# Layer normalisation by block inside attention's steps, in a two-layer attention and mixture-of-experts kernel

## The reference

```python
def _layernorm(x, axis=-1, eps=1e-05):
    m = jnp.mean(x, axis=axis, keepdims=True)
    v = jnp.var(x, axis=axis, keepdims=True)
    return (x - m) / jnp.sqrt(v + eps)

# attention: 16 heads of 16; layer 0 turns q and k by a rotary table, layer 1 has a padding mask
q = query @ Wq.T + bq;  k = ctx @ Wk.T + bk;  v = ctx @ Wv.T + bv
out = softmax(q k^T / 4) v                      # by head
return out @ Wo.T + bo

# experts of layer 0: 8, the best 2 of a row's router logits, and one shared expert of 512
h = (x @ W1[e]) * silu(x @ W3[e]);  y += w[e] * (h @ W2[e])
# experts of layer 1: 16 of 128, the best 4 by sigmoid scores within the best 2 of 4 groups,
# and a shared one of 256

x = x + xattn0(_layernorm(x), ctx);  x = x + ffn0(_layernorm(x))
x = x + xattn1(_layernorm(x), ctx);  x = x + ffn1(_layernorm(x))
```

## Time and profile before

| | us |
|---|---|
| median of 3 runs | 1056.0 |
| the runs | 1051.7, 1056.0, 1056.29 |
| the profiled execution, its own time | 1050.59 |
| its span, first to last instruction | 1048.8 |
| PE busy in the span | 910.7 |
| DVE busy | 671.4 |
| ACT busy | 471.4 |
| POOL busy | 321.3 |

### The profile page before, as it was taken

The page is one execution under the profiler, slowest core; times in us unless marked ns, Lnnn a source line. Parts: engine busy times, 40 slices in busy tenths (PEclk is TensorE's granted clock), DMA queues, the critical chain, the costliest instruction groups (busy, mean ns, idle before and its releaser), DMA issues.

```text
span 1048.8 us, 21972 instructions
## 1 busy us (share of the span) xinstructions
PE 910.7 (87%) x8517; PEld 801.9 (76%) x8517; DVE 671.4 (64%) x1398; ACT 471.4 (45%) x790; POOL 321.3 (31%) x262
## 2 busy tenths in 40 slices
PE   2689888579959999999845999986999999999997
PEld 2578677448859999999834788764778888888886
DVE  5756565477636777777654445546876666666666
ACT  6234445544317777666544554547222222322322
POOL 2321330223745676766421003002112121212210
PEclk9889999889979999999965999997999999999998
DMA  4406600102246888988550000002000000001002
GB/s 138 118 2 186 169 2 2 67 1 86 81 146 182 231 239 231 239 230 236 117 150 21 2 22 2 2 2 61 15 16 19 26 30 15 30 15 30 15 0 81
DMA packets 46115, 85.48 MB, mean 82 GB/s; under 512 B 6240, under 2 KB 33120, under 8 KB 45920
## 3 DMA queue, kind: packets, MB, share of 16 engines
q0 software_dynamic: 14784, 46.44, 16.5%
q1 hardware_dynamic: 31264, 38.09, 12.3%
HBM read 63.73 MB, written 20.79 MB: 81 GB/s over the span
## 4 chain that ended last, share of the span: by engine, by line
PE 66%; DVE 13%; ACT 10%; issue 6%; POOL 3%; DMA 2%; DVEq 0%; POOLq 0%; ACTq 0%
PE bank L1180 36%; PE bank L1216 9%; PE bank L1275 5%; PE bank L1373 3%; PE bank L1379 3%; PE bank L1346 3%; POOL sorted_x L400 2%; ACT prob L635 2%; ACT xn L515 2%; PE bank L1412 2%; PE bank L1422 2%; DMA w_raw<-in_fw,w_idx 1%; DVE qk L1020 1%; DVE rope_b L1020 1%; DVE shift L755 1%
## 5 line engine op out<-in xcount | busy, mean ns | idle before, releaser
L357 POOL TENSOR_TENSOR w_hi<-w_raw,zero_col 128x768 fp32r<-128x768 f32 (+1 forms) x20 | 31.9, 1597 | 357.0 <-PE bank L1216 234.8
L1180 PE MATMUL bank<-xT_hi,w_hi 128*128 128x512 f32 x352 | 139.1, 395 | 2.2 <-DVE hid L958 2.2
L1180 PE MATMUL bank<-xT_lo,w_hi 128*128 128x512 f32 x352 | 139.0, 395 | 0.0
L1180 PE MATMUL bank<-xT_hi,w_lo 128*128 128x512 f32 x352 | 138.8, 394 | 0.0
L945 DVE SCALAR_TENSOR_TENSOR xres<-bank,gate,xres 128x256 f32<-128x256 f32 x320 | 132.7, 475 | 1.2 <-PE bank L1216 1.2
L958 DVE TENSOR_TENSOR hid<-bank,act_sb 128x512 f32<-128x512 f32 x88 | 60.8, 691 | 105.7 <-ACT act_sb L584 105.4
L584 ACT ACTIVATE act_sb<-bank 128x512 f32<-128x512 f32 x88 | 52.6, 598 | 165.9 <-PE bank L1180 165.9
L1180 PE MATMUL bank<-xsT_hi,w_hi 128*128 128x256 f32 x368 | 106.9, 290 | 2.0 <-DVE xsT_lo L912 1.5
L1216 PE MATMUL bank<-w_hi,hid_hi 128*128 128x256 f32 x352 | 100.3, 285 | 6.2 <-DVE hid_lo L966 6.1
L1180 PE MATMUL bank<-xsT_lo,w_hi 128*128 128x256 f32 x368 | 103.8, 282 | 0.0
L1180 PE MATMUL bank<-xsT_hi,w_lo 128*128 128x256 f32 x368 | 103.8, 282 | 0.0
(11 more groups left out here) (199 smaller groups left out, 2277.9 us busy)
## 6 DMA issues: line engine op xcount, KB each, us to landing
w_raw<-in_fw SPq DMA_DIRECT2D x18, 384.0 KB, 3.0
sorted_x<-empty_row SPq DMA_DIRECT2D x2, 2967.0 KB, 20.1
xs<-sorted_x SPq DMA_DIRECT2D x23, 258.0 KB
ctx_raw<-in_ctxT SPq DMA_DIRECT2D x8, 512.0 KB, 4.5
summed<-empty_row SPq DMA_DIRECT2D x1, 2304.0 KB, 26.8
xres<-in_x SPq DMA_DIRECT2D x4, 512.0 KB, 5.9
aw_raw<-in_aw SPq DMA_DIRECT2D x8, 256.0 KB, 5.2
xn_all<-summed SPq DMA_DIRECT2D x4, 512.0 KB, 5.5
```

The source lines that it names most:

```text
L1180: last = nc.tensor.matmul(dst, lh, rh, start=(i == 0), stop=(i == len(pairs) - 1))
```

## The change

The table `build_at` is now written in one pattern: for m = 0, 1, 2 the steps 4m, 4m+1 and 4m+2 make K, Q and V of block m+1 (two items each), and steps 3 and 7 turn the rows of block 2 and 3 for the layer's own normalisation (X0, X1: four transposes each, where other items stand). The functions for a normalisation are split into parts for one block: `deviation`, `normal`, `high` (ACT), `statistics`, `scales`, `low` (DVE) and `rows_turned` (PE). Ahead of attention only blocks 0 and 1 are normalised. The new names of `next_norm(b)` say that steps 12, 13 and 15 turn blocks 0, 1 and 2 for the feed-forward. After attention only block 3 is left. The router's products of blocks 0 and 1 stand in step 16. In the first unit of experts, the products up(0,0) are issued before the last block's transposes; its weights are loaded when attention's K, Q and V are made and split by POOL from step 13 on.

Beside this: the mask's place in memory is moved, so that its load waits for nothing; the four weight loads of layer 1 stand ahead of the loads of the experts' sums; the sort's parts on DVE come with every half step of the shared expert (`between(ls, j)`); the tiles' weights use four semaphores where two were, POOL no longer waits for w_hi before it fetches a tile's weights, and the first two tiles' weights are fetched between the two rounds of scatters.

The core of the diff:

```diff
         def build_at(b):
-            early = {0: (1, K0, K1), 1: (1, Q0, Q1), 2: (1, V0, V1)}
-            if b in early:
-                return early[b]
-            n, s = divmod(b, BLK)
-            if s == 3 and n + 2 < NBLK:
-                return n + 2, K0, V0
-            if s == 0 and n + 1 < NBLK:
-                return n + 1, K1, V1
-            if s == 1 and n + 1 < NBLK:
-                return n + 1, Q0, Q1
+            m, s = divmod(b, BLK)
+            if b == 3 or b == 7:
+                return m + 2, X0, X1
+            if m + 1 < NBLK and s < 3:
+                return (m + 1,) + ((K0, K1), (Q0, Q1), (V0, V1))[s]
             return None
+        def next_norm(b):
+            return {12: 0, 13: 1, 15: 2}.get(b)
...
@@ SP @@
-                sp.wait_ge(a["xadd"], B)
+                sp.wait_ge(a["vps"], 2 * NBLK)
+                sp.wait_ge(a["proj"], 4 * NBLK)
                 for par in range(2):
                     sp.dma_start(w_raw[:, par, 0:768 * J], fw[l][par + (0 if l else SHARED), :, :]).then_inc(f[f"w_in{par}"], 16)
...
@@ POOL, the sort @@
-                    if j:
-                        pool.wait_ge(TS["w_hi"], 2 * j + h - 1)
...
-                for h in range(2):
-                    tile_weights(0, h)
                 pool.wait_ge(LN["ln_xn"], 2 * B)
                 for r in range(2):
                     if r:
+                        for j in range(2):
+                            for h in range(2):
+                                tile_weights(j, h)
                         pool.wait_ge(TS["scatter"], 16 * B)
...
@@ POOL, attention @@
+                    if b == 13:
+                        pool.wait_ge(a["turn"], 12)
+                        split_unit(f, 0, 0, 768 * JT[l])
-                pool.wait_ge(a["xadd"], B)
-                for par in range(2):
-                    split_unit(f, 0, par, 768 * JT[l])
+                pool.wait_ge(a["turn"], B)
+                split_unit(f, 0, 1, 768 * JT[l])
...
@@ ACT, end of step b of attend @@
+                        if made and made[1] == X0:
+                            high(2 * l, made[0])
+                        if next_norm(b) is not None:
+                            high(2 * l + 1, next_norm(b))
+                        if l == 1 and b == 1:
+                            deviation(2, 2)
+                            deviation(2, 3)
-                        if b in (2, 5):
+                        if b in (2, 6):
+                            normal(2 * l, 2 + b // 4)
                             context_high(2 + b // 4)
+                        if b == 10:
+                            if l == 0:
+                                act.wait_ge(s_vset, 3)
+                            deviation(2 * l + 1, 0)
+                            deviation(2 * l + 1, 1)
+                        if b in (11, 12):
+                            normal(2 * l + 1, b - 11)
+                        if b == 13:
+                            deviation(2 * l + 1, 2)
+                        if b == 14:
+                            normal(2 * l + 1, 2)
+                        if b == B:
+                            router_copy(l, 0)
+                            router_copy(l, 1)
...
@@ DVE, end of step b of attend, behind the residual @@
+                        if b in (3, 7):
+                            low(2 * l, 2 + b // 4)
+                        if next_norm(b) is not None:
+                            low(2 * l + 1, next_norm(b))
+                        if l == 1 and b < 2:
+                            tiles_back(2 + b)
+                            statistics(2, 2 + b)
+                        if l == 1 and b == 2:
+                            scales(2, 2)
+                            scales(2, 3)
+                        if l == 0 and b == 6:
+                            first_constants()
+                        if b == 10:
+                            next_statistics(0)
+                            next_statistics(1)
+                        if b == 11:
+                            scales(2 * l + 1, 0)
+                            scales(2 * l + 1, 1)
+                        if b == 13:
+                            next_statistics(2)
+                        if b == 14:
+                            scales(2 * l + 1, 2)
...
@@ PE, attend, behind weighed @@
+                        if next_norm(b) is not None:
+                            pe.wait_ge(a["exp"], NG * b + 1)
+                            rows_turned(2 * l + 1, next_norm(b), 0)
+                        if b == B:
+                            pe.wait_ge(s_wsplit[l], 2)
+                            pe.wait_ge(LN["ln_lo"], 2 * (NBLK * (2 * l + 1) + NBLK - 1))
+                            router_products(0)
...
@@ ACT, then DVE, behind attend @@
-                ln_act(2 * l + 1, (lambda n, t: xn[:, n % 2, t, :]) if l else (lambda n, t: xn_all[:, BLK * n + t, 0:D]))
+                deviation(2 * l + 1, NBLK - 1)
+                router_copy(l, 2)
+                normal(2 * l + 1, NBLK - 1)
+                high(2 * l + 1, NBLK - 1)
+                router_copy(l, 3)
-                ln_dve(2 * l + 1, lambda n: dve.wait_ge(a["xadd"], BLK * (n + 1)))
+                next_statistics(NBLK - 1)
+                scales(2 * l + 1, NBLK - 1)
+                low(2 * l + 1, NBLK - 1)
```

359 lines of the change are left out of this document (197 added, 162 removed).

## The result

The changed kernel is slower: 1065.4 us (median of 7 runs, 1062.7 to 1069.1) against 1054.4 (7 runs, 1051.0 to 1056.3), a ratio of 1.011 with a 95% interval of 1.0084 to 1.0137. Its profiled execution took 1067.61, its span is 1065.8, and the mean granted clock fell from 0.946 to 0.937.

A forecast was written before the change was run, and what follows sets the result against it. TensorE was taken as the apparent bound, with ACT and DVE just behind at step ends. Layers -4.9 and -1.2 plus clock +13.3 gave +7.2: 1057.8 us as profiled, 1063 as median, range 1043 to 1079.

The forecast's parts named there:

- The likeliest case: Whole kernel: late step ends lower TensorE's clock, +3 to +14 us, 1059 to 1070; chance 0.40.
- start of attention: Ahead of attention: fewer blocks normalised first, so it starts earlier, -4.8 us in layer 0 and -12.5 in layer 1.
- behind attention: Feed-forward normalisation and router after attention: one block's chain stays, -15.0 us in layer 0 and -13.1 in layer 1.
- Where the pieces surface: Steps 10 to 14: normalisation work at step ends exceeds ACT's and DVE's slack, +14.6 us in each layer.
- The collision with w_lo: Step 11, layer 0 only: DVE's scales meet GpSimd's weight split, +1.8 us (0 to 2.6).
- The table loads: ACT's loads around each std: costed at nothing; four uncovered switches would add 10.6 us to each layer.
- The clock: Attention: late steps' waits bring TensorE's lower clock, seven net periods of 1.9 us, +13.3 (0 to about 28).
- Steps 15 and 16: End of attention: transposes of block 2 and eight router products, +1.7 us in each layer.
- The signs: Changed profile: first-label wait near 6 us, attention some 20 longer per layer, oT_lo waits of 2.4 or more.
- The clock unchanged: Rival, whole kernel: gain kept without a clock loss, -6 us, 1042 to 1055, centre 1050; chance 0.27.
- The work really hides: Rival, attention: late steps cost only TensorE's own transposes, some 8 us; about -43, 1013; chance 0.08.
- Slower by much: Rival: two half-clock periods per late step or more shift waits, +14 to +28 us, 1070 to 1084; chance 0.17.

The follow-up runs named there:

- e4: The changed kernel with unneeded products added in front of the oT_lo waits of steps 11 to 15, both layers: 1056.1 us.
- e1: The changed kernel with feed-forward statistics, scales, roots and normal of blocks 0 to 2 moved from step ends to where ACT and DVE wait: 1032.4 us.
- e2: As e1, with the attention's own normalisation of blocks 2 and 3 moved as well: 1021.6 us.
- e8: The kernel before, with two added copies on ACT in front of oT_hi in steps 11 to 14, both layers: 1055.8 us in one run.
- e6: The changed kernel with GpSimd's split of the first unit's weights started one step later: 1087.0 us in one run.
- e12: As e11, with unneeded products added in front of the waits of steps 2, 5, 6, 7, 9 and 10 of layer 0: 1020.2 us.
- e11: As e2, with GpSimd's weight fetches in the old order, the first tile's ahead of the first scatter round: 1027.7 us.
- e9: The changed kernel, unedited, measured again in a later session: 1093.9 us, ratio 1.040 to the kernel before.
- e10: The kernel of e2, unedited, measured again in a later session: 1049.2 us, ratio 0.995 to the kernel before.

## Why the prediction was right, point by point

The likeliest case came, at 1065.4 against 1063, and the mechanism was the one forecast: the pieces surface at the ends of steps, and the waits that they make lower TensorE's clock. The number is closer than the sum behind it, which missed 10 us of 17; that part is luck, and so is the session, since the same kernel took 1093.9 in a later one. The terms, each read from the trace of the changed kernel against that of before:

| term | predicted, layer 0 / 1 | measured |
|---|---|---|
| start of attention | -4.8 / -12.5 | -3.9 / -12.0 |
| behind attention (layer 1: to the end of the program) | -15.0 / -13.1 | -14.9 / -12.2 |
| sort, from the ranks to the first tile | -3.4 | -4.0 |
| tile stage | -2.5 | -2.1 |
| behind attention, layer 1, up to the next products of the unit | -13.1 | -13.1 |
| step 11 at full clock (e4) | +4.4 / +2.6 | +4.6 / +2.3 |
| steps 12 to 14 at full clock (e4) | +8.6 / +8.6 | +8.1 / +8.4 |
| steps 15 and 16 at full clock (e4) | +1.7 / +1.7 | +1.6 / +1.6 |
| clock, steps 11 to 14 | within 13.3 for all | +5.2 / +8.1 |
| clock, steps 15 and 16 | within 13.3 for all | +1.6 / +1.4 |
| both attentions in all | +45.2, clock +13.3 | +66.1 |

**Where the pieces surface.** Right, and shown: e1 and e2 keep every instruction and lose 33 and 44 us. The slack was read rightly to 0.3 us (e8). The measured steps 11 to 14 at full clock (e4) are within 0.3 of the sums for single steps, and step 10, put down as +3.4, grew by 3.7 in layer 0 (12.47 against 8.79).

**The collision with w_lo.** Right: shift took 2.16, 2.0 more than its 0.16, where 1.8 was put down; without it the step is 2.0 shorter (e6).

**The table loads.** Put at nothing, and nothing shows. ACT around the loads of step 11 in e1:

```profile
162.97 0.48 ACT L507 ACTIVATE std<-meanvar,eps_col 128x4 f32<-128x4 f32 x2
163.47 1.28 ACT L637 ACT_TABLE_LOAD   x1
164.76 0.69 ACT L637 ACTIVATE prob<-bank,zero_col 128x512 f32<-128x512 f32 x1
```

The load takes 1.28, with no more than 0.02 us free on either side. The 2.66 a switch that the prediction quotes is not seen here, so even four uncovered switches would cost 5.1 a layer and not 10.6.

**The clock.** The mechanism was right and shown by e4 and again by e12 against e11. The price was right too: in steps 11 to 14 seven of the eight ran slow and lost 1.3 to 2.5 each against e4, 13.3 in all and 1.9 apiece, as was put down; the eighth, step 14 of layer 0, ran at 0.99 behind a wait of 2.79. That these seven alone make the forecast's 13.3 is luck, for its seven were to be all the slow periods there are. What was mis-sized is their number. The two steps 15 lost 1.6 and 1.4 more. In layer 0 steps 5, 7 and 9 ran at 0.86, 0.81 and 0.86 and took 12.41, 9.17 and 12.37, against 10.8, 7.8 and 10.8 at full clock (e12), some 4.5 us that were in no term. In layer 1 steps 2 and 3 were slow as forecast (0.87 and 0.84); step 3 took 9.07 against 7.70 at full clock (e2). Waits of 2.2 us as before steps 5, 6, 9 and 10 were there in before too (2.18 in the earlier trace rows), and I took them as harmless; here two of the four were followed by the lower clock. The count of one in four was of layer 0 alone, and a wait of 2.16 at the start of layer 1's attention in before was followed by half clock as well:

```profile
567.08 1.84 PE L1346 MATMUL bank<-k_full,q_half 32*128 32x128 f32 x32 [2.16 <-ACT q_half L626]
```

The same 32 take 1.17 at full clock. Outside attention the clock took some of the gains back: behind the wait of 5.72 before the ranks, and of 2.20 in layer 1, twelve products in a row took about 0.63 apiece where they took about 0.40 before.

```profile
248.24 0.63 PE L1247 MATMUL bank<-xT_hi,w_lo 128*128 128x512 f32 x1
...
749.87 0.80 PE L1247 MATMUL bank<-xT_hi,w_hi 128*128 128x512 f32 x1 [2.20 <-ACT rt L740]
750.47 0.63 PE L1247 MATMUL bank<-xT_hi,w_lo 128*128 128x512 f32 x1
```

That is 2.4 and 1.7 us. In layer 1 the gain of 13.1 at the unit's next products is 12.2 at the end of the program.

**Steps 15 and 16.** The term was right. From scores_turned(15) to the end of attention it was 11.2 and is 14.4 and 14.2, +3.1; but at full clock it is 12.8 (e4), so the pieces cost 1.6 where 1.7 was put down, and the rest is the clock.

**The signs.** The wait for the first labels came out at 1.76 and not near 6. The stretch from the ranks to the first tile gained only 4.0 of those 8.0 us; 2.4 went to the half clock just named. The attentions grew by 31.8 and 34.3, not by some 20. Of the ten waits that the pieces of steps 10 to 14 make, seven were of 2.4 us or more, the others 1.88 and twice 2.09.

**The sum.** +7.2 was forecast for a run like the profiled one, and the two profiled ones differ by 17.0; the medians differ by 11.0. The profiled run of before lies below all seven timed ones, that of the changed kernel among its slower ones; some of the closeness of the forecast to the median is owed to that. Of the missing 10 us some 7.6 lie in the attentions, and the clock of steps 5, 7, 9 and 15 accounts for 7.5; the rest is mainly the starts, which gave 1.4 less, and the 0.9 lost behind attention of layer 1. Inside the attentions smaller misses cancel and were not measured apart. In the chances, a third of 0.27 is 0.09 and not 0.07, which moves 0.02 from faster to within 0.5%.

**The rivals.** "The clock unchanged" falls by the clock of 0.89 in both attentions. "The work really hides" falls for the place where it was put; with the pieces moved (e2) 1021.6 is nearer its 1013 than any other rival's number. "Slower by much" did not come in the first measurement; the 1094 of e9 is beyond it, by a mechanism that was on nobody's list.

## What to carry to other kernels

In a loop that several engines share, look for where each engine waits in a step, not how busy it is: the same four instructions of 2 us cost 2 or more ahead of oT_hi and mostly vanish behind it, where ACT waits. A wait of TensorE can cost more than its length: in this kernel waits of 1.9 to 4.3 us were followed by half clock more often than not, at 1.3 to 2.5 us each, and products that nobody needs were cheaper than the wait. A part of a change that touches transfers should be timed in more than one session before its gain is believed.

## What the runs showed of the hardware that was not expected

TensorE could be held to one matmul in 0.7 to 2.8 us for some 28 us, with no wait that the trace shows, in some sessions and not in others. It began at four indirect fetches between two rounds of indirect scatters; with the fetches ahead of the first round two or three gaps were all.

A wait of 2.2 us decides about the clock only now and then. Step 9 of layer 0 in e2, behind a wait of 2.22, and the same step of the same program in e10, behind one of 2.20:

```profile
138.06:150.51 12.45, 10.25 (x138) 8.87 (x138) 7.75 (x17) 3.46 (x7) 2.53 (x3) 0.86 0.01 3
```

```profile
136.88:147.70 10.82, 8.63 (x138) 7.34 (x138) 7.76 (x17) 3.46 (x7) 2.53 (x3) 1.00 0.01 2
```

The granted clock of the step is 0.86 in the first and 1.00 in the second, and that is 1.6 us.
